# Row 0's shared units and the closings of layers 1 to 3 as products of 64 weight columns

## What is computed

```python
h = relu(ln(x)); x = x + adj @ (h * (u >= 0.1) / 0.9)
h = relu(ln(x)); x = x + l2norm(relu(concat([h, (adj @ h + h) / (deg + 1)]) @ W1 + b1))
h = relu(ln(x)); x = x + (dinv * ((adj + I) * dinv) @ h) @ W2
h = relu(ln(x)); x = x + concat([h, adj @ h / (deg + 1)]) @ W3.T
```

## Time and profile before

| | |
|---|---|
| three runs | 1842.96, 1843.73, 1843.11 us, median 1843.11 |
| the profiled execution | 1843.66 us, its span 1841.8 us |
| PE busy | 1792.9 us, 97% |
| DVE busy | 1483.6 us, 81% |
| DMA | 676.8 MB, 367 GB/s over the span |
| granted TensorE clock, mean | 0.998 |

### The profile page before, as it was taken

How to read it: one execution, slowest core, us unless ns; L and a number is a source line. 1 busy time by engine, 2 the same in 40 slices (tenths; PEclk the granted TensorE clock), 3 DMA queues, 4 the chain that set the end, 5 groups by cost and what they waited for, 6 DMA issues and landing times.

```text
span 1841.8 us, 21052 instructions
## 1 busy us (share of the span) xinstructions
PE 1792.9 (97%) x8376; PEld 643.4 (35%) x8376; DVE 1483.6 (81%) x1545; ACT 102.0 (6%) x270; POOL 9.1 (0%) x23
## 2 busy tenths in 40 slices
PE   5899999999999999999999999999999999999998
PEld 1223333333333333333333333333333333333344
DVE  8999899999997766678878686588888787877754
ACT  0000000000000000100000000110000000000000
POOL 0000000000000000000000000000000000000000
PEclk9999999999999999999999999999999999999999
DMA  9999999999988888198797789499899999999996
GB/s 382 422 421 421 421 421 420 421 421 420 419 342 319 311 291 312 63 390 347 300 400 311 309 355 361 175 397 410 358 421 387 420 387 420 421 388 422 419 422 251
DMA packets 96048, 676.80 MB, mean 367 GB/s; under 512 B 11216, under 2 KB 13264, under 8 KB 14288
## 3 DMA queue, kind: packets, MB, share of 16 engines
q1 hardware_dynamic: 93024, 673.23, 89.7%
q10 hardware_dynamic: 2928, 2.23, 0.4%
HBM read 673.32 MB, written 2.10 MB: 367 GB/s over the span
## 4 chain that ended last, share of the span: by engine, by line
PE 83%; DMA 11%; DVE 5%; issue 0%; SPq 0%; ACT 0%; DVEq 0%
PE acc L789 44%; DMA ring<-stream_in 11%; PE acc L990 4%; PE DEG L946 4%; PE acc L964 4%; PE Z L845 3%; PE acc L819 3%; PE HT L789 2%; PE acc L977 2%; PE acc L1129 2%; PE acc L1069 2%; PE acc L1137 1%; PE acc L1180 1%; PE DEG L1192 1%; DVE ring L1498 1%; PE DEG L1003 1%
## 5 line engine op out<-in xcount | busy, mean ns | idle before, releaser
L789 PE MATMUL acc<-ring,states 128*64 128x512 f32 x3984 | 898.3, 595 | 30.4 <-DMA ring<-stream_in 28.8
L789 PEld LDWEIGHTS acc<-ring,states 128*64 128x64 f32 x3984 | 292.6, 137 | 572.6 <-issue 543.2
L1600 DVE TENSOR_TENSOR row_sum<-row_sum,ring 128x2048 f32<-128x2048 f32 x194 | 444.6, 2292 | 14.5 <-DMA ring<-stream_in 9.5
L946 PE MATMUL DEG<-ring,states 128*64 128x512 f32 x216 | 97.5, 594 | 5.3 <-DMA ring<-stream_in 5.3
L1733 DVE TENSOR_TENSOR ring<-row_totals,ring 128x2048 f32<-128x2048 f32 x27 | 61.9, 2292 | 49.2 <-PE DEG L948 49.0
L948 PE MATMUL DEG<-ring,states 128*64 128x512 f32 x216 | 97.6, 594 | 0.0
L990 PE MATMUL acc<-ring,row_sum 128*64 128x512 f32 x216 | 97.5, 594 | 0.0
L992 PE MATMUL acc<-ring,states 128*64 128x512 f32 x216 | 97.5, 594 | 0.0
L964 PE MATMUL acc<-row_totals,row_sum 128*64 128x512 f32 x216 | 97.1, 592 | 0.0
L966 PE MATMUL acc<-ring,row_sum 128*64 128x512 f32 x216 | 97.1, 592 | 0.0
L789 PE MATMUL acc<-diag,states 128*64 128x512 f32 x336 | 91.1, 594 | 0.9 <-DMA diag<-stream_in 0.5
(11 more groups left out here) (207 smaller groups left out, 2083.2 us busy)
## 6 DMA issues: line engine op xcount, KB each, us to landing
ring<-stream_in SPq DMA_DIRECT2D x610, 1024.0 KB, 14.0
diag<-stream_in SPq DMA_DIRECT2D x28, 1024.0 KB, 13.6
x<-x_in SPq DMA_DIRECT2D x4, 512.0 KB, 6.7
y<-u_in SPq DMA_DIRECT2D x4, 512.0 KB, 8.4
x_out<-x ACTq DMA_DIRECT2D x16, 128.0 KB, 6.9
below<-w_in ACTq DMA_DIRECT2D x6, 16.0 KB, 5.7
bias<-b_in ACTq DMA_DIRECT2D x1, 32.0 KB, 9.1
```

The costliest lines, as they stand in the source:

```text
L789: return nc.tensor.matmul(half_of(bank, half), h[layer % 2][:, J], moving, start=start, stop=stop)
L946: nc.tensor.matmul(down("P2"), h[0][:, a12[2] * TPR + k], source_tile(slot(a12), k), start=i == 0 and k == 0, stop=False)
L1600: nc.vector.tensor_tensor(row_sum[:, :], before, slot(key)[:, :], ALU.add).then_inc(unit_summed, 1 if count > 1 else 2)
```

## The change

`both_at_once` issues, for each tile of the unit, two products of 64 weight columns, the states of layer 2 into the lower half of the bank and those of layer 1 into the upper. `finish`, in layers 1 to 3, takes each tile of 128 nodes as two halves of 64: weights of 64 columns, the outcome into partitions 0 to 63 or 64 to 127 of the same columns of `Z`. The operands, sums and semaphores are the same.

```diff
--- before.py
+++ after.py
@@ -816,9 +816,8 @@
 
                 for k in range(TPR):
                     J = key[2] * TPR + k
-                    done = nc.tensor.matmul(acc[bank][:, :], states[:, J * 2 * F:(J + 1) * 2 * F],
-                                            source_tile(slot(key), k), start=first and k == 0,
-                                            stop=last and k == TPR - 1)
+                    mm(bank, 0, 2, J, source_tile(slot(key), k), first and k == 0, last and k == TPR - 1)
+                    done = mm(bank, 1, 1, J, source_tile(slot(key), k), first and k == 0, last and k == TPR - 1)
                 done.then_inc(unit_freed, 1)
 
             def finish(layer, b):
@@ -842,8 +841,10 @@
                     if layer == 0:
                         mm_z = nc.tensor.transpose(Z[:, t * P:(t + 1) * P], gathered_sums, ident[:, :])
                     else:
-                        mm_z = nc.tensor.matmul(Z[:, t * F:(t + 1) * F], gathered_sums, below[:, layer - 1, :],
-                                                start=True, stop=True)
+                        for half in (0, 1):
+                            nodes = slice(half * F, (half + 1) * F)
+                            mm_z = nc.tensor.matmul(Z[nodes, t * F:(t + 1) * F], gathered_sums[:, nodes],
+                                                    below[:, layer - 1, :], start=True, stop=True)
                 mm_z.then_inc(z_done, 1)
 
             def pick(b):
```

## The result

The changed kernel takes **1816.6 us** (median of 4 runs, 1816.13 to 1817.69) against 1843.03 for the kernel before (1842.66 to 1843.73): ratio 0.9855, 95% interval 0.9843 to 0.9866. The forecast was 1816. The profiled execution took 1816.89 us with a span of 1815.1.

What follows compares the result with a forecast made beforehand. TensorE (PE), 97% busy, was taken as the bound. Gains of 12.6 us up to phase 3's pairs and 5.9 in them put the last landing at 1804.7; a 9.9 tail ends at 1814.6, so 1816 us forecast (1811 to 1821, chance 0.72).

Steps and rivals of the forecast that it cites:

- the new closing: Closings of layers 1 to 3 as 8 side-by-side pairs of passes: 0.45 us in place of 1.18.
- one with a turning: Closing followed by the turning of states, which stays 128 wide: 1.62 us before, 0.44 gained.
- its split: Wide closing's 1.18 us taken as 1.03 to the next product plus 0.15 for changes of weight width.
- Head of phase 2: From 755 to 804 us, five closings and the first shared unit: 2.8 us gained, limited by states from DVE.
- Four changes of pair: In phase 2, 1.27 us gained at each, capped at 1.05 at the second by DVE's wait: 4.9 us.
- Pairs of phase 3: First five changes of pair each restart the load queue 1.17 us earlier: 5.9 us gained.
- Last landing: Last load lands at 1804.7 us in place of 1823.2, making DMA the bound of the last rows.
- Tail: From last landing to span's end, set by the DVE chain, last closing at the lower clock: 9.9 us.
- Side by side: Rival: short products' halves do not run side by side; closing 0.89 us, kernel 1831.5 us; chance 0.12.
- The slower case: Rival: each pass has a floor of 0.111 us, none overlap; closing 1.78, kernel 1871 us; chance 0.05.
- the change does nothing: Rival: the 0.15 per width change is a record's artefact and closings wait for DVE: 1843 us; chance 0.03.
- Waits: Rival: half of the 5.9 and a third of the 12.6 us are lost in waits: 1823 us; chance 0.08.

Runs made afterwards that it cites:

- the doubled closings: Two runs with every closing's products issued twice: narrow ones in the changed kernel, 1832.44 us; wide ones in the kernel before, 1887.16 us.
- closings alone: Changed kernel with the shared units back to one product of 128 columns, only the closings of layers 1 to 3 in halves: 1820.08 us.
- layer 0's transposes split: Changed kernel with the turnings of states and also layer 0's 64 transposes into Z issued as halves: 1819.09 us.
- the run in the lower half: Changed kernel with both halves of a closing sent to Z's lower 64 partitions, so they cannot run side by side: 1833.93 us.
- halves apart: Changed kernel with the loop over halves put around the loop over tiles in each closing: 1823.01 us.
- the turnings' run: Changed kernel with the turnings of states issued as halves of 64 columns by matmul in place of transposes: 1817.91 us.
- layer 3 only: Kernel before with only layer 3's 16 closings as two halves side by side: 1835.38 us.
- double narrow passes: Changed kernel with every closing's halves issued twice over: 1832.44 us.
- layer 3 wide: Changed kernel with layer 3's 16 closings again one product of 128 columns: 1823.64 us.
- units alone: Changed kernel with closings back to one product of 128 columns, only row 0's shared units as 64-column products: 1842.09 us.
- the quarters: Changed kernel with each closing's products in four quarters of 32 nodes in place of two halves of 64: 1822.57 us.
- double wide products: Kernel before with every closing's wide products issued twice over: 1887.16 us.

## Why the prediction was right

- **Prices.** Foretold 0.45 for the new closing, measured 0.47; 3.43 for a narrow unit, measured 3.43; 0.73 off a closing, measured 4.62 - 3.90 = 0.72; 0.44 off one with a turning, measured 1.62 - 1.18 = 0.44, where the 1.62 holds a 0.15 that was read elsewhere; the issues of the loads move by 0.41 to 0.43 at these places. The total was right though its split was not: 0.28 and not 0.15 of a wide closing is change of width. It did no harm because each gain was taken as a difference of whole prices. The Trainium skill (TensorEngine Tiling (Array Packing), Key Properties) states that changing the tiling mode drains TensorE; the doubled closings agree in that a part of the price does not grow with the number of products, 0.28 us for a round trip here.
- **Up to phase 3.** Head of phase 2: 2.8 foretold, load 292 is issued 2.91 earlier. Four changes of pair 4.9 and the one shared unit inside: load 371 is 7.96 earlier, against 2.8 + 4.9 + 0.34 = 8.0. Read where the advance stands still between two changes, the four bring 1.29, 1.05, 1.27 and 1.29, foretold 1.27, 1.05, 1.27 and 1.27: the cap by DVE's wait at the second is there too. By load 396, 12.61 against 12.6.
- **Pairs of phase 3.** 5.9 foretold, 5.89 measured between loads 396 and 560. The single changes, read in the same way, bring 1.17, 1.14, 1.14, 1.44 and 1.00 where 1.17 was foretold; the last two are off by 0.27 and -0.17, which the sum hides.
- **Last landing.** 1804.7 foretold, 1806.21 measured: this term was 1.5 us off. Load 636 still lands 18.01 earlier than before, 637 only 17.00. In the half microsecond from 1803.0 the DMA view shows the load queue and, beside it, a fetch of instructions:

```profile
q1 hardware_dynamic: 15, 0.11, 50.5%
q8 instruction: 1, 0.02, 13.3%
```

  It is one packet of 16 KB (1.18 MB over 72 packets), as long as 13.3% of 16 engines' 0.5 us, 1.06 us on one engine. Each load lands in 16 parts, and the trace records each. Fifteen parts of the last load had landed by 1805.09, and the sixteenth came 1.12 later, about the length of the fetch; in the load before it the last two parts are 0.25 apart. Nine of the fourteen kernels have one gap of over 3.1 us among their last 38 landings (3.46 to 4.21 us); the other five, the kernel before among them, have none. At each of the nine the last part comes 0.88 to 1.49 behind the one before it, and a fetch of 16 KB starts 2.3 to 4.5 us ahead of the landing: at 1803.47 in the changed kernel, at 1806.97 (landing 1809.37) with closings alone, at 1787.87 (1792.35) with layer 0's transposes split. Most fetches leave no gap. After that at 1784.84 in the changed kernel one part of the load that lands at 1789.21 has moved back by some 0.8 us, but not behind the last. So a fetch seems to hold up one of 16 parts, and to cost time only where that part comes last. This is the likely cause of 1.0 of the 1.5 us: which engine served the fetch is not seen, and no run moved it alone. The other 0.5 stays open.
- **Tail.** 9.9 foretold from the last landing, 8.9 measured. The step that the last closing has the lower clock level failed: it ran at the upper one, 0.80 to z where I put 1.25. (With layer 0's transposes split it did run at the lower one, and took 1.24 to z, 1813.78 to 1815.02, so the price was right and the level was not.) And the closing of row 13 came 1.83 after the landing, not 2.4: with the unit late, DVE's fold was ready (1807.40) and PE's own 1.74 counted. The two offset 1.0 of the 1.5 us by which the landing was late, so 1816 for 1816.6 owes about 1 us to luck.
- **The rivals.** Side by side fell to the run in the lower half: without pairs the closing costs 0.94 and the kernel 1833.9, where the rival put 0.89 and 1831.5. The Trainium skill's 62 ns per matmul with hardware decode off (TensorE: Matmul & The Clock Gate, What happens when you issue a matmul) is not seen: 16 passes start within 0.47 us, 29 ns apiece. The slower case would have needed 0.074 a pass; even unpaired they take 0.059. That the change does nothing fell with the time itself. Waits took nothing beyond what was counted, up to load 560.

## What to carry to other kernels

Price a short product by the distance between its neighbours' starts, width changes included, and take the difference of whole prices: here less than two thirds of the gain was in the product itself. A few stray products of another width cost 0.28 us each time between narrow ones, and the gain of removing them comes only when both neighbours have one width (1.1 us against 3.5 for the same edit). And follow a gain through the transfers it restarts: the last point where the queue ran empty decided when the last data landed, and work saved behind it counted only until PE caught up.

## What the runs showed that I had not expected

- The two halves of the array each keep their own order only: a product started before three passes ahead of it in the program that belong to the other half. The Trainium skill (TensorE: Matmul & The Clock Gate, Packing small matmuls) says that matmuls start and end in program order and that a weight load overlaps running products only where the row groups differ. The measurement decides otherwise here, for two column halves over the same 128 rows. The starts of the run with halves apart (1760.32 before 1760.37) break the order, and in the changed kernel a closing's first two loads start at 1749.30, 0.42 before its first product, while the unit's last products run.
- 32-column passes bring back a change of width against 64-column ones, 0.16 us in front and 0.11 behind. The 32 passes in four quarters themselves take what 16 in two halves take, so finer splitting gained nothing.
- After nearly the same wait, 2.49 to 2.52 us, the last closing had the upper clock level in six of the kernels (0.69 long in the changed one, the closings-alone run, the turnings' run and that with layer 3 only; 1.15 with double narrow passes, 1.10 with layer 3 wide). It had the lower (granted 0.50) in five: the kernel before and that with units alone (1.97 for the wide closing), the halves apart (1.60), the quarters (1.08) and layer 0's transposes split (1.12). With double wide products (3.27) and in the lower-half run (1.18) the level fell while it ran. Nothing in these rows tells them apart, so a tail should be foretold with both.
